# Landmark attention with a mixture of experts: a new order on VectorE, GpSimd and ScalarE in the query stage

## The chip, the core and the metric

The kernel runs on one core of a Trainium2 chip. The metric is the device time of one execution in microseconds (us), lower is better. Engines are TensorE (PE in the profile), VectorE (DVE), ScalarE (ACT), GpSimd (POOL) and SyncE (SP), which issues the DMAs here. Each runs its own list of instructions in order; semaphores tie them together.

## What is computed

Eight sequences of 2048 tokens with 256 channels go through a kernel attention with 64 landmarks per head (16 heads) and a layer norm, and then through a top-2 mixture of 8 experts and another layer norm:

```python
Phi_Q = jnp.exp(-C_Q / temperature)        # squared distances of queries to 64 landmarks
...
Y = jnp.linalg.solve(W_kernel, Z)
out_unnorm = jnp.einsum('bhnk,bhkd->bhnd', Phi_Q, Y)
norm = jnp.einsum('bhnk,bhko->bhno', Phi_Q, jnp.linalg.solve(W_kernel, Phi_K_sum))
out = out_unnorm / jnp.maximum(norm, 1e-10)
...
x = _layernorm(x + attn(x))
# ffn: logits = x @ Wg.T + bg; top 2 of 8 experts, softmax of the two logits
all_out = jnp.einsum('nd,ehd->neh', xf, We) + be
out = jnp.sum(sel * gate_w[:, :, None], axis=1)
x = _layernorm(x + out)
```

## The kernel before

The key stage (some 680 us) builds the landmark sums and inverses. It isn't touched. The query stage behind it works through 32 chunks of 512 tokens, four chunks a batch. A chunk is four tiles of 128 tokens. All its engine lists are written out by hand, so the order of the calls in the code is the order on the engine.

The stage is a software pipeline. One turn of the loop handles three chunks at once: p is in the experts, c = p + 1 in normalisation and gates, q = p + 2 in distances and attention.

TensorE computes 16 expert products per chunk (`experts(p, n)`, n = 4t + pair for tile t and pair of experts), each of six matrix products (L299 to L301) into bank 2 or 3 in turn. Between them stand: the distances of q (L1606), the attention of q in two halves (L1636), the output projection, the transposes (L1662), the gate logits of c (L1674), the norms of queries (L1417), the transposes of the gates (L1683) and the bias term (L1694), which closes the chunk.

A tile's expert results are gathered so. VectorE takes the first pair out of bank 2 with the gates (`combine`, L1298 and L1299) into y_out, which frees the bank for the third pair. ScalarE weighs the other three pairs (`weigh`, L841) into three buffers; there are two sets of these, for even and odd tiles. GpSimd adds the three up (`sum_parts`, L561 to L563). VectorE adds that sum to y_out and takes its statistics (`finish`, L1306 to L1310). GpSimd turns statistics into coefficients (`ln2`, through L527 to L530, the second being a power). ScalarE applies them (`result`, L849). SyncE stores two tiles at a time.

VectorE has much more to do: it clamps phi (`q_clamp`, L1177), which the attention of that half waits for; it takes reciprocals of the norms in two halves and multiplies (`norm_begin`, L1199 and L1200; `norm_end`, L1206 and L1209); it adds the residual and takes the first norm's statistics (`residual_stats`, L1218 to L1226); it splits x1 (`x1_lo`, L1234) and the queries (L969) into high and low parts; it turns logits into gates (`gates_begin`, L1245 to L1259, with a cast at L1256; `gates_end`, L1266 to L1275). GpSimd also makes low parts (`split_lo`, L536; `attn_lo`, L542), adds the output bias to x_tok (`residual`, L549) and makes the first norm's coefficients (`ln1`). ScalarE also exponentiates the distances (L786), rounds the attention for `attn_lo` (`attn_hi`, L794) and normalises x1 (L808).

## Time and profile before

| | |
|---|---|
| median of 3 runs | 2023.41 us |
| lowest, highest | 2021.66, 2028.81 us |
| the profiled execution, its own time | 2032.55 us |
| its span | 2030.8 us |
| granted TensorE clock over the span | 0.952 |
| busy over the span: TensorE, VectorE, ScalarE, GpSimd | 1811.0, 1534.3, 1225.9, 931.6 us |

The trace shows for each instruction its start, its length and, in brackets, the idle time in front of it on its engine with what ended that. A chunk of the query stage takes 40 to 44 us. The chunk that is followed below begins with expert product 0 on TensorE at 1200.27 us and ends where the next begins, at 1240.18.

### The profile page before, as it was taken

Reading aid. Unit: us, or ns where it says so; the run is one execution under the profiler, and the core shown is the slowest. Engines: PE = TensorE matmul, PEld = TensorE weight load, DVE = VectorE, ACT = ScalarE, POOL = GpSimd, SP = SyncE. Lnnn points to the kernel's source line nnn. Section 1 sums busy time; section 2 is a strip of 40 time slices with the busy share of each in tenths; the row PEclk is TensorE's granted clock in tenths of the full one; section 3 lists DMA queues with packets and bytes.
Section 4 is the critical chain, followed back from the end, with each engine's and each line's share of the span. In section 5 each row is a group of like instructions: output and inputs, shape, how many; then the busy total and the mean of one; then the engine's idle time right before and its main releaser. Section 6 shows DMA issues by size and latency. Waiting matters only on the chain.

```text
span 2030.8 us, 42773 instructions
## 1 busy us (share of the span) xinstructions
PE 1811.0 (89%) x16312; PEld 1369.3 (67%) x16312; DVE 1534.3 (76%) x3316; ACT 1225.9 (60%) x2411; POOL 931.6 (46%) x1179
## 2 busy tenths in 40 slices
PE   4668999989884899999999999999999999999997
PEld 3267778878772676676667767667676667766765
DVE  5668854888434788888888888887888878888874
ACT  2246665766655466568557566655855756675553
POOL 2300000000001376666666677656766666666666
PEclk8689999999996899999999999999999999999999
DMA  2586696766955233333243333333324333333300
GB/s 81 78 179 144 159 199 142 179 160 166 196 146 142 68 82 96 89 90 88 73 109 93 80 94 78 96 87 94 89 73 105 87 91 90 77 86 92 89 27 21
DMA packets 210753, 214.02 MB, mean 105 GB/s; under 512 B 59228, under 2 KB 142580, under 8 KB 210292
## 3 DMA queue, kind: packets, MB, share of 16 engines
q1 hardware_dynamic: 210356, 210.75, 43.0%
q8 instruction: 129, 2.11, 0.4%
q14 instruction: 76, 0.62, 0.1%
q0 software_dynamic: 192, 0.52, 0.1%
HBM read 61.26 MB, written 23.59 MB: 42 GB/s over the span
## 4 chain that ended last, share of the span: by engine, by line
PE 42%; DVE 26%; POOL 12%; issue 10%; SPq 5%; DMA 3%; ACT 2%; DVEq 0%; POOLq 0%; ACTq 0%
PE bank L299 9%; PE bank L300 9%; PE bank L301 9%; POOL x_tok L549 3%; PE bank L1606 3%; PE bank L1496 3%; PE bank L1636 2%; POOL part_x L562 2%; POOL part_x L561 2%; DVE phi L1177 2%; PE bank L1512 2%; DVE nrm L1199 2%; PE bank L1497 2%; DVE if L1256 2%; DVE inversion L1053 2%
## 5 line engine op out<-in xcount | busy, mean ns | idle before, releaser
L299 PE MATMUL bank<-weh,x1h 128*128 128x512 f32 x1024 | 433.3, 423 | 36.8 <-DVE y_out L1299 17.6
L300 PE MATMUL bank<-weh,x1l 128*128 128x512 f32 x1024 | 408.9, 399 | 0.0
L301 PE MATMUL bank<-wel,x1h 128*128 128x512 f32 x1024 | 408.6, 399 | 0.0
L549 POOL TENSOR_TENSOR x_tok<-x_tok,bo_sb 128x1024 f32<-128x1024 f32 x32 | 76.8, 2401 | 531.7 <-DMA x_tok<-in_x 531.7
L841 ACT ACTIVATE part_x<-bank,gate 128x256 f32<-128x256 f32 x512 | 211.3, 477 | 171.0 <-PE bank L301 166.9
L299 PEld LDWEIGHTS bank<-weh,x1h 128*128 128x128 f32 x1024 | 195.2, 191 | 156.3 <-issue 60.5
L786 ACT ACTIVATE phi<-bank,nlt_cur,invt 128x512 f32<-128x512 f32 x256 | 187.0, 793 | 86.5 <-PE bank L1606 86.5
L301 PEld LDWEIGHTS bank<-wel,x1h 128*128 128x128 f32 x1024 | 195.3, 191 | 47.8
L641 ACT ACTIVATE phi<-bank,invt 128x512 f32<-128x512 f32 x256 | 162.6, 684 | 105.2 <-PE bank L1497 105.0
L300 PEld LDWEIGHTS bank<-weh,x1l 128*128 128x128 f32 x1024 | 195.9, 191 | 34.2
L561 POOL TENSOR_TENSOR part_x<-part_x 128x512 f32<-128x512 f32 x128 | 177.8, 1389 | 32.6 <-ACT part L841 32.4
L1025 DVE TENSOR_SCALAR phi<-phi,phi_max,phi_min 128x1024 f32<-128x1024 f32 x128 | 103.7, 810 | 105.3 <-ACT phi L641 105.2
L542 POOL TENSOR_TENSOR attn_l<-attn,attn_h 128x512 fp32r<-128x512 f32 x64 | 85.3, 1333 | 210.2 <-ACT attn_h L794 210.2
L841 ACT ACTIVATE part<-bank,gate 128x256 f32<-128x256 f32 x256 | 107.7, 479 | 121.1 <-PE bank L301 120.7
L1496 PE MATMUL bank<-l_hh,k_hl 128*128 128x256 f32 x512 | 145.9, 316 | 39.1 <-DMA k_ha<-key_aug 26.5
L562 POOL TENSOR_TENSOR part_x<-part_x,part 128x512 f32<-128x512 f32 x128 | 173.0, 1351 | 10.0
L1177 DVE TENSOR_SCALAR phi<-phi,phi_max,phi_min 128x1024 f32<-128x1024 f32 x128 | 144.2, 1162 | 19.1 <-ACT phi L786 18.7
L1636 PE MATMUL bank<-phi,y_cur 128*32 128x512 f32 x1024 | 133.2, 641 | 12.6 <-issue 8.7
L1496 PEld LDWEIGHTS bank<-l_hh,k_hl 128*128 128x128 f32 x512 | 100.2, 196 | 54.8 <-DMA k_hl<-kl 33.6
L1497 PE MATMUL bank<-l_lo,k_ha 128*128 128x256 f32 x512 | 132.2, 289 | 0.0
L527 POOL TENSOR_TENSOR ve<-mv,cst 128x1 f32<-128x1 f32 (+1 forms) x160 | 46.6, 291 | 185.3 <-DVE mv L1310 112.9
L299 PE MATMUL bank<-xh,wh 128*128 128x512 f32 x260 | 107.4, 413 | 13.2 <-DVE xl L1045 6.9
(198 smaller groups left out, 4465.5 us busy)
## 6 DMA issues: line engine op xcount, KB each, us to landing
x_raw<-in_xT SPq DMA_DIRECT2D x64, 512.0 KB, 4.4
q_stack<-kh SPq DMA_DIRECT2D x256, 128.0 KB, 2.4
x_tok<-in_x SPq DMA_DIRECT2D x32, 512.0 KB, 3.9
q_stack<-kl SPq DMA_DIRECT2D x128, 128.0 KB, 2.4
q_stack<-key_aug SPq DMA_DIRECT2D x128, 128.0 KB, 2.5
k_hl<-attn_h SPq DMA_DIRECT2D x32, 256.0 KB
k_ha<-attn_h SPq DMA_DIRECT2D x32, 256.0 KB
k_hl<-attn_l SPq DMA_DIRECT2D x32, 256.0 KB
```

What stands on the lines that cost most here:

```text
L299: nc.tensor.matmul(outp, ah, bh, start=first, stop=False)
L300: nc.tensor.matmul(outp, al, bh, start=False, stop=False)
L301: return nc.tensor.matmul(outp, ah, bl, start=False, stop=last)
L561: own.then(nc.gpsimd.tensor_tensor(a[0], a[0], a[1], ALU.add))
L562: own.then(nc.gpsimd.tensor_tensor(a[0], a[0], a[2], ALU.add))
L641: nc.scalar.activation(phi[:, n], bank[6 + s][:], ACT.Exp, scale=invt[:]).then_inc(exp_done, 1)
L786: nc.scalar.activation(phi[:, i], bank[6 + i % 2][:], ACT.Exp, bias=nlt_cur[:, i:i + 1], scale=invt[:]).then_inc(qexp_done, 1)
L841: last = nc.scalar.activation(parts[t % 2][q - 1][:, u * D:(u + 1) * D], bank[2 + q % 2][:, u * D:(u + 1) * D], ACT.Copy, scale=gate[at][: ...
L1177: V.tensor_scalar(two, two, phi_max[:], phi_min[:], ALU.min, ALU.max).then_inc(qphi_ready, 2)
L1496: mm(dst, k_hl[at][:, g, tok], wide(hh), start=True, stop=False)
L1497: last = mm(dst, k_ha[at][:, g, tok], wide(lo), start=False, stop=True)
L1636: last = mm(dst[32 * j:32 * j + 32, :], y_cur[:, 4 * half + j, n:n + 32], phi[:, 4 * half + j], start=True, stop=True)
```

## The change

On GpSimd the first norm's coefficients (`ln1(c)`) move behind `sum_parts(p, 0)`; `sum_parts(p, 1)` and `attn_lo(q, 0)` move ahead of `ln2(p, 0)` and of `residual(q)`; and `ln2` handles two tiles in one call: tiles 0 and 1 in one, tiles 2 and 3 of the chunk before in another. On VectorE, `combine(p, 0)` now stands ahead of `finish(p-1, 2)`, and `finish(p-1, 3)` stands behind the residual and `combine(p, 1)`. On ScalarE `result(p, 0)` stands next to `result(p, 1)`, and `result` for tiles 2 and 3 is put into the next turn, behind `weigh(p, 7)`. SyncE stores tiles 2 and 3 in the next turn. TensorE's list is as before.

```diff
@@ SyncE
+            def store_rows(p, half):
+                sp.wait_ge(res_ready, TPC * p + 2 * half + 2)
+                sp.dma_start(out_v[p, :, 2 * half:2 * half + 2],
+                             y_out[p % 2][:, 2 * half:2 * half + 2]).then_inc(res_stored[p % 2][half], 16)
...
+                    if p:
+                        store_rows(p - 1, 1)
                     stack_queries(p + 3)
...
-                    for half in range(2):
-                        sp.wait_ge(res_ready, TPC * p + 2 * half + 2)
...
+                    store_rows(p, 0)
@@ GpSimd
             def ln2(p, t):
-                pool.wait_ge(ln2_stats, TPC * p + t + 1)
-                layernorm_coefs(mv2, ve2, rs2, nt2, nm2, slice(t, t + 1)).then_inc(ln2_coef, 1)
+                pool.wait_ge(ln2_stats, TPC * p + t + 2)
+                layernorm_coefs(mv2, ve2, rs2, nt2, nm2, slice(t, t + 2)).then_inc(ln2_coef, 2)
...
                     sum_parts(p, 0)
+                    ln1(c)
+                    if p:
+                        ln2(p - 1, 2)
                     split_lo(q + 1, 1)
+                    sum_parts(p, 1)
+                    attn_lo(q, 0)
                     ln2(p, 0)
                     residual(q)
-                    sum_parts(p, 1)
-                    ln2(p, 1)
-                    attn_lo(q, 0)
                     sum_parts(p, 2)
                     attn_lo(q, 1)
                     sum_parts(p, 3)
-                    ln2(p, 2)
-                    ln2(p, 3)
-                    ln1(c + 1)
@@ ScalarE
-                if not first:
-                    result(p - 1, 2)
                 q_exps(p + 2, range(2, 4))
...
                     weigh(p, 7, me)
+                    if p:
+                        result(p - 1, 2)
+                        result(p - 1, 3)
                     x1_hi(c, nxt)
...
                     gate_exp(c)
-                    result(p, 0)
...
                     weigh(p, 14, me)
+                    result(p, 0)
                     result(p, 1)
...
-                    result(p, 3)
@@ VectorE
                 add_bias(p, at)
+                combine(p, 0, at)
                 if not first:
                     finish(p - 1, 2)
-                combine(p, 0, at)
+                residual_stats(p + 1, 1 - at)
+                combine(p, 1, at)
                 if not first:
                     finish(p - 1, 3)
-                residual_stats(p + 1, 1 - at)
-                combine(p, 1, at)
                 q_clamp(p + 2, range(0, 2))
```

The line numbers of the changed kernel are 5 to 7 higher. On GpSimd the middle of a turn, from behind `split_lo`, reads before as follows: coefficients of tile 0, x_tok (`residual`), the sum of tile 1, coefficients of tile 1, `attn_lo`.

```order
L536 TENSOR_TENSOR xl1<-x_raw0,xh1 128x1024 [waits xqh_ready]
L527 TENSOR_TENSOR ve2<-mv2,cst 128x1 [waits ln2_stats]
...
L549 TENSOR_TENSOR x_tok<-x_tok,bo_sb 128x1024 [waits xt_loaded]
L561 TENSOR_TENSOR part_x<-part_x 128x512 [waits part_ready]
L562 TENSOR_TENSOR part_x<-part_x,part 128x512 [waits pool_step]
L563 TENSOR_TENSOR part_x<-part_x 128x256 [waits pool_step]
...
L542 TENSOR_TENSOR attn_l<-attn,attn_h 128x512 [waits attnh_ready]
L561 TENSOR_TENSOR part_x<-part_x 128x512 [waits part_ready]
```

The same place in the changed kernel, from the coefficients of the two norms ahead of `split_lo` (ve1 is `ln1`, ve2 is `ln2`):

```order
L533 TENSOR_TENSOR ve1<-mv1,cst 128x4 [waits ln1_stats]
...
L533 TENSOR_TENSOR ve2<-mv2,cst 128x2 [waits ln2_stats]
...
L542 TENSOR_TENSOR xl1<-x_raw0,xh1 128x1024 [waits xqh_ready]
L567 TENSOR_TENSOR part_x<-part_x 128x512 [waits part_ready]
...
L548 TENSOR_TENSOR attn_l<-attn,attn_h 128x512 [waits attnh_ready]
L533 TENSOR_TENSOR ve2<-mv2,cst 128x2 [waits ln2_stats]
...
L555 TENSOR_TENSOR x_tok<-x_tok,bo_sb 128x1024 [waits xt_loaded]
L567 TENSOR_TENSOR part_x<-part_x 128x512 [waits part_ready]
```

Both norms' coefficients of eight instructions now stand ahead of xl1, and the x_tok addition stands where `attn_lo` stood, directly behind the coefficients of tile 1.

On VectorE, from the residual to the attention's norms (L1199), before:

```order
L1306 TENSOR_TENSOR y_out<-y_out,part_x 128x256 [waits comb_done,part_sum]
L1308 BN_STATS st2<-y_out 128x6 [waits acc_done]
L1310 BN_AGGR mv2<-st2 128x2 [waits dve_step]
L1218 TENSOR_TENSOR x1_0<-bank0,x_tok 128x256 [waits wo_done,xb_ready]
...
L1298 SCALAR_TENSOR_TENSOR y_spare<-bank2,gate1,x1_1 128x256 [waits res_stored10,be_added,ffn_done]
L1299 SCALAR_TENSOR_TENSOR y_spare<-bank2,gate1,y_spare 128x256 [waits dve_step]
L1177 TENSOR_SCALAR phi<-phi,phi_max,phi_min 128x1024 [waits qexp_done] x3
L1199 TENSOR_SCALAR nrm<-bank5 128x512 [waits attn_ready,out_done]
```

And in the changed kernel:

```order
L1225 TENSOR_TENSOR x1_0<-bank0,x_tok 128x256 [waits wo_done,xb_ready]
...
L1305 SCALAR_TENSOR_TENSOR y_spare<-bank2,gate1,x1_1 128x256 [waits res_stored10,be_added,ffn_done]
L1306 SCALAR_TENSOR_TENSOR y_spare<-bank2,gate1,y_spare 128x256 [waits dve_step]
L1313 TENSOR_TENSOR y_out<-y_out,part_x 128x256 [waits comb_done,part_sum]
L1315 BN_STATS st2<-y_out 128x6 [waits acc_done]
L1317 BN_AGGR mv2<-st2 128x2 [waits dve_step]
L1184 TENSOR_SCALAR phi<-phi,phi_max,phi_min 128x1024 [waits qexp_done] x3
L1206 TENSOR_SCALAR nrm<-bank5 128x512 [waits attn_ready,out_done]
```

The three instructions of `finish(p-1, 3)` have moved from in front of the residual to between the combination of tile 1 and the clamps.

## Rows read from the trace of the kernel before

**Rows 1.** A query-stage stretch: busy PE, PEld, DVE, ACT, POOL; clock, DMA

```profile
1200.00:1400.00 200.00, 191.57 (x1085) 140.47 (x1084) 164.62 (x395) 129.83 (x272) 137.85 (x177) 0.98 0.36 91
```

**Rows 2.** TensorE's waits, 720 to 1985 us: total, times, longest

```profile
PE bank L299 <- DVE y_out L1299: 15.1, 10, 2.1
PE bank L299 <- DVE y_spare L1299: 13.9, 13, 2.1
PE bank L1683 <- DVE g_st L1275: 13.2, 14, 1.4
PE bank L1636 <- issue: 8.7, 7, 2.5
PE bank L1674 <- DVE x1l L1234: 5.2, 14, 1.9
...
PE bank L1636 <- DVE phi L1177: 2.9, 4, 0.8
```

**Rows 3.** VectorE's waits in the same stretch

```profile
DVE y_spare L1306 <- POOL part_x L563: 52.4, 30, 2.9
DVE y_out L1306 <- POOL part_x L563: 48.3, 31, 4.5
```

**Rows 4.** Timeline of TensorE in one chunk: start, length, idle before

```profile
1215.00 1.92 PE L1636 MATMUL bank<-phi,y_cur 128*32 128x512 f32 x16
...
1226.19 0.17 PE L1674 MATMUL bank<-wg_s,x1h 128*128 128x16 f32 x1
...
1235.84 0.50 PE L299 MATMUL bank<-weh,x1h 128*128 128x512 f32 x1 [0.78 <-DVE y_out L1299]
```

**Rows 5.** Timeline of VectorE in the same chunk

```profile
1206.11 0.42 DVE L1306 TENSOR_TENSOR y_spare<-y_spare,part_x 128x256 f32<-128x256 f32 x1 [1.64 <-POOL part_x L563]
...
1211.37 0.48 DVE L1298 SCALAR_TENSOR_TENSOR y_out<-bank,gate,x 128x256 f32<-128x256 f32 x1 [0.75 <-PE bank L301]
...
1212.29 4.22 DVE L1177 TENSOR_SCALAR phi<-phi,phi_max,phi_min 128x1024 f32<-128x1024 f32 x3
...
1219.39 0.37 DVE L1306 TENSOR_TENSOR y_out<-y_out,part_x 128x256 f32<-128x256 f32 x1
...
1224.49 1.28 DVE L1234 TENSOR_TENSOR x1l<-bank,x1h 128x512 fp32r<-128x512 f32 x2
...
1228.31 0.43 DVE L1306 TENSOR_TENSOR y_out<-y_out,part_x 128x256 f32<-128x256 f32 x1 [1.22 <-POOL part_x L563]
...
1231.14 1.10 DVE L1256 CAST if<-i 128x8 f32<-128x8 uint32 x1
```

**Rows 6.** Timeline of GpSimd in the same chunk

```profile
1212.51 1.75 POOL L561 TENSOR_TENSOR part_x<-part_x 128x512 f32<-128x512 f32 x1
...
1217.07 2.40 POOL L536 TENSOR_TENSOR xl<-x_raw,xh 128x1024 fp32r<-128x1024 f32 x1
...
1222.44 2.41 POOL L549 TENSOR_TENSOR x_tok<-x_tok,bo_sb 128x1024 f32<-128x1024 f32 x1
...
1230.91 1.30 POOL L542 TENSOR_TENSOR attn_l<-attn,attn_h 128x512 fp32r<-128x512 f32 x1
```

**Rows 7.** Timeline, two other chunks: a GpSimd and two VectorE instructions

```profile
1257.75 2.40 POOL L536 TENSOR_TENSOR xl<-x_raw,xh 128x1024 fp32r<-128x1024 f32 x1
...
1259.30 1.13 DVE L1306 TENSOR_TENSOR y_spare<-y_spare,part_x 128x256 f32<-128x256 f32 x1
...
1359.63 1.26 DVE L1258 TENSOR_TENSOR oh<-cst,if 128x32 f32<-128x32 f32 x1
```

**Rows 8.** Timeline of ScalarE in the chunk followed

```profile
1210.65 0.85 ACT L841 ACTIVATE part<-bank,gate 128x256 f32<-128x256 f32 x2
...
1227.12 0.63 ACT L794 ACTIVATE attn_h<-attn 128x512 fp32r<-128x512 f32 x1
```

**Rows 9.** The power of the coefficients in the query stage: ns min/median/max, forms

```profile
L528 POOL TENSOR_TENSOR rs<-ve,cst x159: 545/550/1032, 700.3 to 2026.4; 128x1 f32<-128x1 f32 x128, 128x4 f32<-128x4 f32 x31
```

**Rows 10.** TensorE's busy time and clock, one stretch of two us

```profile
1644.00:1646.00 2.00, 2.00 (x10) 0.50 0.00 0
```

More of the change, by code:

```diff
@@ L478, in turn @@
                         sp.dma_start(x_raw[0][:], xT_v[:, :, bass.ds((p + 4) * CH, CH)]).then_inc(xq_loaded, 16)
-                    for half in range(2):
-                        sp.wait_ge(res_ready, TPC * p + 2 * half + 2)
-                        sp.dma_start(out_v[bass.ds(p, 1), :, 2 * half:2 * half + 2].rearrange("a p t d -> (a p) t d"),
-                                     y_out[p % 2][:, 2 * half:2 * half + 2]).then_inc(res_stored[p % 2][half], 16)
+                    store_rows(p, 0)
             for b in range(BATCH - 1):
@@ L486, in _ @@
             turn(BATCH - 1)
+            store_rows(NCH - 1, 1)
             for i in range(2):
@@ L576, in _ @@
             attn_lo(1, 1)
-            ln1(1)
             def turn(b):
@@ L600, in _ @@
             turn(BATCH - 1)
+            ln2(NCH - 1, 2)
         @block.scalar
@@ L882, in _, with first_tile @@
             attn_hi(1, 1)
-            def first_tile(p, at, first=False, new_batch=None):
+            def first_tile(p, at, new_batch=None):
                 q_exps(p + 2, range(0, 2))
@@ L890, in first_tile @@
                     z_landmark_major(new_batch)
-                if not first:
-                    result(p - 1, 2)
                 q_exps(p + 2, range(2, 4))
                 weigh(p, 3, at)
-            first_tile(0, 0, True)
+            first_tile(0, 0)
             def turn(b):
@@ L938, in _ @@
             turn(BATCH - 1)
+            result(NCH - 1, 2)
+            result(NCH - 1, 3)
         @block.vector
```

## The prediction

> **What bounds the kernel now.** I read the stretches first, then TensorE's waits, then one chunk's timeline on each engine. In the query stage (1200 to 1400 us) TensorE is busy for 191.57 us of 200, at a clock of 0.98, and VectorE for 164.62 [rows 1]. TensorE sets the time, and only its gaps can be won or lost. From 720 to 1985 us, some 30 chunks, it waited 15.1 + 13.9 us for VectorE's combination (L1299), 13.2 for the gates (L1683's releaser L1275), 8.7 + 2.9 before the attention products (L1636) and 5.2 before the gate logits (L1674) [rows 2]: 59.0 us, 1.97 per chunk. If all of it went, the kernel would take some 1964 us.
>
> VectorE waited 52.4 + 48.3 us for GpSimd's sums before `finish` (L1306) [rows 3], 3.3 per chunk. Those are the waits that the change goes for. They aren't TensorE's, so I followed one chunk. It begins on TensorE at 1200.27. Attention of half 0 runs from 1215.00 to 1216.92; I call its end E. The gate logits come at 1226.19 (E + 9.27), and expert product 14 could have started at 1235.84 - 0.78 = 1235.06 (E + 18.14) but waited for the combination of tile 3 [rows 4]. So each chunk has two legs. In leg A VectorE clamps phi just in time for the attention: TensorE went from distances to attention without an idle mark. In leg B VectorE starts at E and must reach `combine(p, 3)` by E + 18.14; it took 18.9.
>
> **Leg A: what is moved in front of the clamps.** In the tile-0 and tile-1 part `finish(p-1, 3)` stood before the residual. There it waited 1.64 us in the chunk shown, but in a place with slack: VectorE still waited 0.75 for TensorE before `combine(p, 1)` at 1211.37. This combination can't come earlier, since it needs expert product 4. Now `finish(p-1, 3)` stands behind it and in front of the three clamps that began at 1212.29 [rows 5]. It costs 0.43 for the addition and, to its last statistic, 1.2 in all. The clamps start at 1213.5. The first two free the attention. In the chunk shown they ended at 1215.0 because a GpSimd addition (1212.51, 1.75 long) held the second one back [rows 6]; GpSimd is again inside a sum there, so I keep that pattern. Attention starts 1.15 late: 1.15 us of TensorE wait, where L1636 now has 11.6 / 30 = 0.39. Bounds: 0 if the clamps then run unhindered, 1.7 if the second also meets a long addition.
>
> **Leg B: what goes and what comes.** Going: `sum_parts(p, 1)` is moved ahead of the coefficients and of the residual addition (2.41 us at 1222.44 [rows 6]), so `finish(p, 1)` loses its wait of 1.22 before 1228.31 [rows 5]. Alone this puts combine 3 at E + 17.7, and the expert wait is gone.
>
> Coming: GpSimd's instructions now lie elsewhere, and the trace shows that some VectorE instructions stand still while GpSimd runs one. The addition L1306 at 1259.30 took 1.13, ending 0.28 after GpSimd's `split_lo` (1257.75 + 2.40), against 0.37 at 1219.39. The tiny cast L1256 at 1231.14 took 1.10 and ended with `attn_lo` (1230.91 + 1.30). L1258, an operation on 32 numbers per partition at 1359.63, took 1.26 [rows 5 to 7]. A collision costs what is left of GpSimd's instruction, whatever VectorE's own length.
> The Trainium skill, page "SBUF — State Buffer", section "Who interferes with whom", says the same: two-input additions and casts in VectorE's fast modes block fully, they don't share. Were the port shared instead, each collision worked out below would cost half, the waits per chunk would be near 2.5 and the sum 2023 + 0.5 x 30 = 2038; by these rows it is the full block.
>
> The new GpSimd order, in the chunk's times: ScalarE's third weighing ended at 1211.5 [rows 8] and loses a 0.6 normalisation ahead of it, so `sum_parts(p, 0)` runs 1211.0 to 1215.5 (4.56 as before, 1212.51 to 1217.07 [rows 6]). Then `ln1(c)`, four short instructions whose power takes 1.03 for four columns [rows 9]: 1.85, plus 0.2 behind a clamp, to 1217.6. Then the two-column `ln2(p-1, 2)`: the power is 0.55 for one column and 1.03 for four, so I take 0.7, 1.45 in all, to 1219.05. Then `split_lo` to 1221.5. The new E is 1218.07, and `finish(p, 0)` comes 2.47 behind it as now (1219.39 - 1216.92), at 1220.54: it stands until 1221.8, 0.9 lost. GpSimd takes `sum_parts(p, 1)` straight behind, and its first addition holds the clamp of pairs 6 and 7 for 0.5. VectorE is now 1.4 late.
> - Gate logits: `x1_lo` ended at 1225.77, E + 8.85 [rows 5], and would end at E + 10.25; TensorE wants it at E + 9.27. Wait 1.0, now 0.17.
> - `finish(p, 1)`: it would come at E + 10.17 (1228.31 - 1.22) + 1.4 = 11.6. `attn_lo` follows ScalarE's rounding, 1227.75 or E + 10.83 [rows 8], and runs to E + 12.15. Blocked again; its statistics end at E + 13.15, where the chunk shown had 12.6. The wait removed is back as collisions.
> - The cast: before, GpSimd's coefficients started as soon as the statistics ended, and `attn_lo` started 2.60 after L1306 did; the cast came at 2.83. In the place of `attn_lo` now stands the residual addition, and the pow of two columns adds 0.15: 2.75 against 2.83. The cast thus stands behind 2.40 us, not 1.30: 1.3 more than in the chunk shown (if it slips in ahead, L1258 stands in its stead). Behind it `sum_parts(p, 2)` may catch L1258 for another 1.1, as at 1359.63.
>
> Combine 3 ends 6.3 behind the statistics in the chunk shown, now 7.6 to 8.7: E + 20.7 to 21.8. TensorE, 1.0 later by the logits, wants it at E + 19.15. Wait 1.55 to 2.65. The gates follow in the same order and cost no more (0.44 per chunk today goes into that wait).
>
> **The rest.** Coefficients for two tiles at a time save GpSimd 8 of 16 short instructions per chunk, some 2 us by [rows 9], but GpSimd isn't what TensorE waits for: 0, apart from the times above. On ScalarE two normalisations move behind the seventh weighing (1.1 us while it waits for the transposes; 0, at most 0.3 at x1_hi) and `result(p, 0)` next to `result(p, 1)` (0.5 before the last weighing; 0.6 of slack before product 1). On SP's queue the store of half 1 no longer stands ahead of the next x_tok load; it now stands ahead of `stack_queries` and waits for `result(p-1, 3)`, near E + 3.8, while the stacking needs rounded queries that come after the logits' time, E + 9: 0. Behind the last chunk both normalisations and the store follow the same last sum as before: within 1 us.
>
> **The sum.** TensorE's waits per chunk: 1.15 + 1.0 + 1.55 to 2.65 = 3.7 to 4.8, against 1.97. That is 1.7 to 2.8 more in 30 chunks, 52 to 85 us; middle 68. The profiled execution took 2032.55, 9 above the median of the timed ones; I put the difference on the median: 2023.4 + 68 = **2091**.
>
> **Rivals.**
> 1. The collisions don't line up. This is a race with a threshold: if `finish(p, 1)` is less than 0.7 late (collisions of `finish(p, 0)` and the clamp together), it passes before `attn_lo` starts. Then the coefficients wait for `attn_lo`, and the cast is through before the residual. Leg B's waits vanish, leg A's 1.15 stays: 0.8 less per chunk, 2023.4 - 25 = 1998; with a part of the chunks so, up to 2010. For it: VectorE's 3.3 us of waits do go. Against: `split_lo` would have to end 0.7 earlier than worked out. Chance 0.25.
> 2. Only the last collision is missed (the cast is free). Waits 1.15 + 1.0 + 0.2: 0.4 more, 2035; with half of leg A's delay lost too, no change. Chance 0.15.
> 3. The clock. In the chunk where TensorE waited 2.5 us before the attention, it ran at half its clock (0.50, that is 1.2 GHz) from 1644 to 1646 [rows 10]. Such stretches cost some 1.7 us each. With a wait near 2.5 in every chunk, a stretch in each costs up to 1.7 more for perhaps half of them in sight: 2091 + 25 = 2116. Chance 0.08.
> The Trainium skill, page "TensorE: Matmul & The Clock Gate", section "HAM oscillation — how this bites in real kernels", describes this: a kernel that waits in every tile can have its clock dropped in every tile. By that rule rival 3 would be the rule; the trace shows waits of 2.08 without a drop behind them.
>
> **Chances and range.** Forecast (2068 to 2108) 0.52. An effect under 0.5% (10 us) can't be told from none here. Faster by more than that: rival 1, 0.26. Within: 0.10, the lower part of rival 2. Slower: 0.64. The range must reach rival 1, whose time is 1998, and stops at 2112, leaving out the worst of rival 3. The forecast alone has 2068 to 2108.
>
> **What would show it.** Right: VectorE's wait for part_x before L1306 nearly gone; TensorE's wait before the attention near 1 us in most chunks; L1256's mean up from 1.1 towards 2.3; L1306 of `finish(p, 0)` over 1 us; waits before the gate logits and product 14. Wrong: L1256 under 0.5 and L1306 under 0.5 throughout (rival 1); an attention that starts without a wait, which would mean that the clamps aren't the last thing before it.

## The result, and the profile after

| | before | changed |
|---|---|---|
| median (lowest to highest) of 4 runs, us | 2024.39 (2021.66 to 2028.81) | 2072.22 (2068.61 to 2077.56) |
| span of the profiled execution, us | 2030.8 | 2068.9 |
| granted TensorE clock over the span | 0.952 | 0.947 |

The ratio is 1.0236, 95% interval 1.0206 to 1.0266: the change makes the kernel 2.4% slower. Lines of the changed kernel are 5 to 7 higher: L1306 is now the second instruction of `combine`, L1313 the addition of `finish`, L1184 the clamp, L1263 the cast, L1265 and L1266 the two comparisons behind it.

The same stretch as in [rows 1], with the same columns (TensorE, weight loads, VectorE, ScalarE and GpSimd busy; clock; DMA):

```profile
1200.00:1400.00 200.00, 185.50 (x1026) 136.07 (x1026) 164.81 (x379) 119.43 (x254) 116.89 (x121) 0.96 0.35 90
```

TensorE is busy for 6 us less of 200, and issues 1026 matrix products where it issued 1085. VectorE is as busy as before: it does less work in longer instructions. What TensorE waits for, 720 to 2020 us (total, times, longest), against [rows 2]:

```profile
PE bank L1681 <- DVE x1l L1241: 26.7, 22, 1.9
PE bank L299 <- DVE y_spare L1306: 15.4, 9, 2.4
PE bank L1643 <- DVE y_cur L1196: 15.4, 7, 2.2
PE bank L1690 <- DVE g_st L1282: 14.8, 17, 1.4
PE bank L1643 <- DVE phi L1184: 12.6, 22, 0.7
PE bank L299 <- DVE y_out L1306: 10.8, 5, 2.9
```

VectorE's waits for part_x, 100.7 us in [rows 3], are gone from the head of its list. It now waits for TensorE, which is itself late because of VectorE, as the list above shows:

```profile
DVE x L1225 <- PE bank L301: 53.8, 60, 2.1
DVE y_out L1305 <- PE bank L301: 41.2, 20, 3.2
DVE nrm L1206 <- PE bank L1643: 41.2, 29, 2.7
```

Now one chunk of the kind that the prediction followed. On TensorE, against [rows 4], three places with an idle mark:

```profile
1228.09 1.93 PE L1643 MATMUL bank<-phi,y_cur 128*32 128x512 f32 x16 [0.58 <-DVE phi L1184]
...
1240.61 0.28 PE L1681 MATMUL bank<-wg_s,x1h 128*128 128x16 f32 x1 [1.17 <-DVE x1l L1241]
...
1251.87 0.50 PE L299 MATMUL bank<-weh,x1h 128*128 128x512 f32 x1 [2.28 <-DVE y_out L1306]
```

VectorE there, against [rows 5]:

```profile
1224.76 0.41 DVE L1313 TENSOR_TENSOR y_spare<-y_spare,part_x 128x256 f32<-128x256 f32 x1
...
1225.88 2.88 DVE L1184 TENSOR_SCALAR phi<-phi,phi_max,phi_min 128x1024 f32<-128x1024 f32 x3
...
1232.48 1.88 DVE L1313 TENSOR_TENSOR y_out<-y_out,part_x 128x256 f32<-128x256 f32 x1
...
1241.80 0.70 DVE L1313 TENSOR_TENSOR y_out<-y_out,part_x 128x256 f32<-128x256 f32 x1
...
1244.89 0.17 DVE L1263 CAST if<-i 128x8 f32<-128x8 uint32 x1
1245.10 2.27 DVE L1265 TENSOR_TENSOR oh<-cst,if 128x32 f32<-128x32 f32 x1
1247.29 1.32 DVE L1266 TENSOR_TENSOR oh<-cst,if 128x32 f32<-128x32 f32 x1
```

GpSimd there, against [rows 6]:

```profile
1231.68 2.40 POOL L542 TENSOR_TENSOR xl<-x_raw,xh 128x1024 fp32r<-128x1024 f32 x1
...
1240.92 1.30 POOL L548 TENSOR_TENSOR attn_l<-attn,attn_h 128x512 fp32r<-128x512 f32 x1 [2.86 <-ACT attn_h L799]
1243.37 0.20 POOL L533 TENSOR_TENSOR ve<-mv,cst 128x2 f32<-128x2 f32 x1 [1.15 <-DVE mv L1317]
1243.64 0.71 POOL L534 TENSOR_TENSOR rs<-ve,cst 128x2 f32<-128x2 f32 x1
...
1244.92 2.40 POOL L555 TENSOR_TENSOR x_tok<-x_tok,bo_sb 128x1024 f32<-128x1024 f32 x1
1247.28 1.29 POOL L567 TENSOR_TENSOR part_x<-part_x 128x512 f32<-128x512 f32 x1
```

Read the last two fences side by side, by ends. L1313 starts 0.80 behind `split_lo` and ends at 1234.36, 0.28 after `split_lo` ends (1234.08). L1265, 32 numbers per partition, starts 0.18 behind the x_tok addition and ends at 1247.37, 0.05 after that ends. L1266 does the same with the first addition of the sum: 1248.61 against 1248.57. Beyond what they take when unhindered (0.41, 0.19 and 0.18), the three cost 1.5 + 2.1 + 1.1 us. Not every VectorE instruction does that: the norms' copy out of PSUM (1248.53, 0.68) and a reciprocal (1249.24, 1.75) ran at their usual length beside the rest of the same sum, and so did the two instructions of a combination out of PSUM (1235.99, 0.47 and 1236.50, 0.48) beside the sum of tile 1.

How regular it is, the first comparison over all chunks (ns: minimum, median, maximum):

```profile
L1265 DVE TENSOR_TENSOR oh<-cst,if x32: 191/2242/2281, 676.4 to 2026.3; 128x32 f32<-128x32 f32 x32
```

Seven chunks, those in which the next batch's landmark values are taken in between the clamps, are another kind. There `finish(p, 1)` slips in ahead of `attn_lo` and the comparison is free, on VectorE:

```profile
1332.02 0.41 DVE L1313 TENSOR_TENSOR y_out<-y_out,part_x 128x256 f32<-128x256 f32 x1
...
1335.03 0.20 DVE L1265 TENSOR_TENSOR oh<-cst,if 128x32 f32<-128x32 f32 x1
1338.71 0.45 DVE L1273 TENSOR_SCALAR gs<-ge 128x4 f32<-128x4 f32 x1
1339.41 1.13 DVE L1275 TENSOR_TENSOR gw<-gw,ge 128x4 f32<-128x4 f32 x1
```

and the collisions sit one place further on, in `gates_end` (L1273 on), on operations on four numbers per partition, under the sum of tile 2. TensorE waits in these chunks for y_cur, 2.2 us in each of the seven, and some 1.0 for the gates.

The other chunks differ behind L1265. Where the sum of tile 2 then catches L1266 as well, as above, TensorE waits some 2.3 us for the combination. Where L1266 slips through (0.18), the sum catches `gates_end` instead in nine chunks, and TensorE waits 0.7 for the gates; in four it catches next to nothing, and the combination costs 1.1.

**A book for all kernels.** In the table, "waits" is the sum of TensorE's listed waits from 720 us to the end of the stage. "Clock" is my sum of (1 - granted clock) x 2 us over all stretches of two us from 690 us on. "Rest" is the span less both. The clock column also counts stretches in which TensorE waits or has ended (3 to 6 us of it lie behind the last product, and in some rows the last stretch, 1.0 us, is left out), so 1 us in it means nothing.

| kernel | ratio to before (95%) | span | waits | clock | rest |
|---|---|---|---|---|---|
| before | 1 | 2030.8 | 68.7 | 25.5 | 1936.6 |
| changed | 1.0236 (1.0206 to 1.0266) | 2068.9 | 100.2 | 38.7 | 1930.0 |
| r_late | 1.0742 (1.0705 to 1.0779) | 2173.9 | 145.1 | 112.5 | 1916.3 |
| r_half | 1.0313 (1.0277 to 1.0350) | 2091.0 | 113.0 | 51.3 | 1926.7 |
| r_gap | 1.0111 (1.0062 to 1.0160) | 2050.6 | 83.5 | 39.2 | 1927.9 |
| dve_before | 1.0178 (1.0138 to 1.0217) | 2056.6 | 80.1 | 44.5 | 1932.0 |
| clamp_first | 1.0212 (1.0181 to 1.0243) | 2066.3 | 85.1 | 31.4 | 1949.8 |
| fin_mid | 1.0196 (1.0170 to 1.0222) | 2058.8 | 80.1 | 49.3 | 1929.4 |
| gap_split | 1.0038 (1.0022 to 1.0055) | 2030.5 | 83.5 | 24.6 | 1922.4 |
| gap_split_mid | 0.9845 (0.9818 to 0.9873) | 1987.4 | 48.2 | 8.8 | 1930.4 |
| one_tile | 0.9872 (0.9838 to 0.9907) | 1999.3 | 48.6 | 16.6 | 1934.1 |
| gates_clear | 0.9652 (0.9630 to 0.9675) | 1958.1 | 22.0 | 6.7 | 1929.4 |
| after_clear | 1.0115 (1.0080 to 1.0150) | 2037.2 | 66.2 | 48.8 | 1922.2 |
| before_clear | 0.9861 (0.9827 to 0.9896) | 1989.1 | 43.6 | 15.4 | 1930.1 |

For twelve of the fourteen the rest is 1922 to 1937. So nearly all of each difference is in the two columns in the middle: of the change's 38.1 us of span, 31.5 are waits and 13.2 clock, and the rest fell by 6.6.

The 31.5 are made up of 21.5 more before the gate logits, 16.4 more before the attention (15.4 + 12.6 in place of 8.7 + 2.9) and 3.1 more for the gates, less 6.2 for the combinations (26.2 in place of 32.4 to the end of the stage) and 3.3 for ScalarE and the DMA.

### The profile page after: what moved, and what is told of

It is laid out like the page before. It is cut to its first block, busy times and chain, and to the rows that moved or that the text cites. A ratio compares the mean times of both kernels' runs of the same rounds, so it can differ in the third digit from the quotient of the medians.

```text
span 2068.9 us, 42581 instructions
## 1 busy us (share of the span) xinstructions
PE 1819.7 (88%) x16312; PEld 1373.4 (66%) x16312; DVE 1569.4 (76%) x3316; ACT 1227.7 (59%) x2411; POOL 874.2 (42%) x923
## 4 chain that ended last, share of the span: by engine, by line
PE 47%; DVE 31%; issue 12%; SPq 4%; ACT 2%; DMA 2%; POOL 1%; DVEq 0%; ACTq 0%; POOLq 0%
PE bank L299 10%; PE bank L300 9%; PE bank L301 9%; PE bank L1643 4%; PE bank L1503 2%; DVE y_spare L1313 2%; DVE nrm L1213 2%; PE bank L1519 2%; PE bank L1613 2%; DVE phi L1184 2%; PE bank L1504 2%; DVE inversion L1060 2%; DVE phi L1032 2%; DVE kl L976 2%; DVE st L1315 2%
## 5 line engine op out<-in xcount | busy, mean ns | idle before, releaser
L299 PE MATMUL bank<-weh,x1h 128*128 128x512 f32 x1024 | 432.9, 423 | 28.3 <-DVE y_spare L1306 15.4
L568 POOL TENSOR_TENSOR part_x<-part_x,part 128x512 f32<-128x512 f32 x128 | 178.7, 1396 | 10.0
L1032 DVE TENSOR_SCALAR phi<-phi,phi_max,phi_min 128x1024 f32<-128x1024 f32 x128 | 103.7, 810 | 100.5 <-ACT phi L646 100.3
L1643 PE MATMUL bank<-phi,y_cur 128*32 128x512 f32 x1024 | 141.9, 678 | 28.5 <-DVE y_cur L1196 15.9
L1184 DVE TENSOR_SCALAR phi<-phi,phi_max,phi_min 128x1024 f32<-128x1024 f32 x128 | 121.3, 981 | 18.3 <-ACT phi L791 17.7
L299 PE MATMUL bank<-xh,wh 128*128 128x512 f32 x260 | 107.8, 415 | 13.2 <-DVE xl L1052 6.9
L1207 DVE RECIPROCAL nrm<-nrm 128x256 f32<-128x256 f32 x64 | 112.2, 1753 | 2.2
```

The lines of the kernel that those rows point to most:

```text
L299: nc.tensor.matmul(outp, ah, bh, start=first, stop=False)
L568: own.then(nc.gpsimd.tensor_tensor(a[0], a[0], a[2], ALU.add))
L1184: V.tensor_scalar(two, two, phi_max[:], phi_min[:], ALU.min, ALU.max).then_inc(qphi_ready, 2)
L1643: last = mm(dst[32 * j:32 * j + 32, :], y_cur[:, 4 * half + j, n:n + 32], phi[:, 4 * half + j], start=True, stop=True)
```

## Experiments

The theory: the change costs what VectorE stands still behind GpSimd's long instructions. The main rival: it costs what the moved `finish(p-1, 3)` and the new order on VectorE make late by themselves. All edits are to the changed kernel unless said otherwise.

### The x_tok addition: smaller, or elsewhere

Three ways to free L1265. **r_half** cuts the addition in two, the halves on either side of the sum:

```diff
-                    residual(q)
+                    half_residual(q, 0)
                     sum_parts(p, 2)
+                    half_residual(q, 1)
```

> The changed kernel with the x_tok addition cut into two halves of 512 columns, one where the whole stood, one behind the sum of tile 2. The total work on GpSimd grows only by one instruction's fixed cost. Theory (the hold lasts for what is left of the GpSimd instruction): L1265 falls by half, to about 1.1 us, followed by a hold of up to 1.3 on the next one as before; VectorE is 1.1 us earlier per chunk, time about 2072 - 25 = 2047. If VectorE's loss didn't depend on the length of the instruction it meets, the median would stay at 2.2 and the time at 2072.

Measured: 2092.26 us. The dose came out: this comparison, L1281 here, took half of its 2242 ns.

```profile
L1281 DVE TENSOR_TENSOR oh<-cst,if x32: 191/1142/1168, 671.9 to 2047.4; 128x32 f32<-128x32 f32 x32
```

The time did not fall to the 2047 that I expected: the second half now stood in front of the gates, where TensorE's wait rose from 14.8 to

```profile
PE bank L1706 <- DVE g_st L1298: 50.3, 29, 2.5
```

**r_late** puts the whole addition behind the sum of tile 2:

```diff
-                    residual(q)
                     sum_parts(p, 2)
+                    residual(q)
```

> The changed kernel with GpSimd's x_tok addition (residual of q, 2.40 us) moved behind the sum of tile 2. Theory (collisions with GpSimd's long addition hold VectorE's small gate operations, 2.27 us in 23 of 30 chunks): L1265's median falls from 2.24 to about 0.2, TensorE's waits before product 14 (15.4 + 10.8 us) and for g_st (14.8) go almost entirely, the waits before the gate logits (26.7) and the attention (28) stay; time 2072 - 40 = 2032. Rival (VectorE is late in leg B for other reasons, its wait is only named here): waits unchanged, 2072. Rival (the place behind the sum collides with something as costly): 2060 or more.

Measured: 2175.82 us, the slowest of all, and 144 off what I expected. L1265 was free (median 192 ns). The collision had moved whole, to an instruction of `gates_end`, median 2303 ns. Ahead of it the sum held L1273 for 1.27 as well:

```profile
L1276 DVE TENSOR_TENSOR oh<-oh,gw x32: 191/2303/2304, 676.3 to 2134.3; 128x32 f32<-128x32 f32 x32
```

Behind it TensorE waited for the gates 28 times up to 2020 us, 2.8 us each. One such wait, and the clock in the stretches from 1246 on (TensorE busy, weight loads, VectorE, ScalarE, GpSimd, clock, DMA):

```profile
1246.24 0.61 PE L1690 MATMUL bank<-cst,g_st 128*24 128x128 f32 x4 [2.82 <-DVE g_st L1282]
```

```profile
1246.00:1248.00 2.00, 1.76 (x9) 1.43 (x10) 1.93 (x6) 1.11 (x3) 0.00 (x0) 0.81 0.03 8
1248.00:1250.00 2.00, 2.00 (x7) 1.20 (x5) 1.49 (x3) 2.00 (x6) 0.00 (x0) 0.50 0.44 102
1250.00:1252.00 2.00, 2.00 (x6) 1.54 (x6) 1.18 (x4) 0.40 (x1) 1.52 (x2) 0.50 0.95 180
1252.00:1254.00 2.00, 2.00 (x6) 1.60 (x5) 0.92 (x3) 0.00 (x0) 1.92 (x2) 0.50 0.77 224
1254.00:1256.00 2.00, 2.00 (x13) 1.70 (x12) 1.26 (x4) 0.79 (x2) 1.17 (x2) 0.99 0.78 281
```

Six us at 1.2 GHz in place of 2.4: this wait of 2.8 cost about 3.4 more in clock. Over the stage the clock column went from 38.7 to 112.5. So of r_late's 105 us of span above the changed kernel, 45 are waits and 74 clock (the rest fell by 14).

The waits of 2.8 us are only half of that clock. Low stretches stand behind 17 of the 28, at 1.7 or 3.4 us each; with the last one of 3.3 us they make up 55 of the 112.5. Another 43 stand behind the waits of some 1.2 us before the gate logits, such as this one:

```profile
1231.41 0.28 PE L1681 MATMUL bank<-wg_s,x1h 128*128 128x16 f32 x1 [1.18 <-DVE x1l L1241]
```

```profile
1234.00:1236.00 2.00, 2.00 (x16) 0.36 (x8) 1.72 (x19) 0.00 (x0) 1.30 (x4) 0.50 0.87 201
```

In r_late all 21 of these have a low stretch behind them, in the changed kernel 10 of 22. The length of the last wait alone therefore doesn't decide whether the clock falls; what else does, these runs don't show.

**r_gap** puts it where GpSimd was idle for 2.86 us, ahead of `attn_lo`:

```diff
                     sum_parts(p, 1)
+                    residual(q)
                     attn_lo(q, 0)
                     ln2(p, 0)
-                    residual(q)
                     sum_parts(p, 2)
```

> The changed kernel with the x_tok addition between the sum of tile 1 and attn_lo, where GpSimd stood idle for 2.87 us in each chunk while VectorE runs reciprocals and operations with an input from PSUM. Theory of collisions: no VectorE instruction of the two-input SBUF or cast kind meets the 2.40 us, L1265 falls to 0.2 and L1273 to L1276 meet at most the sum of tile 2; the waits before product 14 go, the one for g_st is under 1 us, so the clock isn't dropped as in the run with the addition behind the sum (waits of 2.8, clock 0.916). Gate logits (1.17) and attention (0.57) waits stay. Time 2072 - 35 = 2037, 2020 to 2045. If the clock dropped for another reason than long waits, it would stay near 0.92 and the time above 2100.

Measured: 2047.22 us, 25 below the changed kernel, 10 above my middle value and 2 outside my range. L1265 took 191 ns (median) and the waits for the combination fell from 26.2 us to

```profile
PE bank L299 <- DVE y_spare L1306: 0.6, 1, 0.6
```

The sum of tile 2 had moved 2.4 us forward, though, and met L1273 (median 1278 ns in place of 456): the wait for the gates rose from 14.8 to 23.6. Three runs, one answer: a collision costs what is left of GpSimd's instruction, and when that instruction moves, the cost moves to whatever stands there. Only a place where VectorE has nothing that collides would be free.

### What stands before the attention

**dve_before** gives VectorE its old order:

```diff
+                if not first:
+                    finish(p - 1, 2)
                 combine(p, 0, at)
                 if not first:
-                    finish(p - 1, 2)
+                    finish(p - 1, 3)
                 residual_stats(p + 1, 1 - at)
                 combine(p, 1, at)
-                if not first:
-                    finish(p - 1, 3)
```

> VectorE's list as in the kernel before; GpSimd, ScalarE and SyncE as in the changed kernel. Theory (leg A's loss comes from finish(p-1, 3) in front of the clamps): the wait before the attention for phi, 12.6 us in 22 waits of 0.57, falls below 5 us; VectorE waits again before L1306. Leg B is unchanged or slightly worse, since split_lo comes as late as before and E earlier: gate logits and product 14 keep their waits. Time 2060 to 2072. Rival (the VectorE order is the main cause of the slowdown): 2035 or less.

**clamp_first** moves `finish(p-1, 3)` alone, behind the second half's clamps:

```diff
                 combine(p, 1, at)
-                if not first:
-                    finish(p - 1, 3)
                 q_clamp(p + 2, range(0, 2))
@@ in the turn
                     q_clamp(q, range(2, 4))
+                    if p:
+                        finish(p - 1, 3)
@@ behind the last turn
+            finish(NCH - 1, 3)
```

> The changed kernel with finish(p-1, 3) behind the second clamp instead of in front of the first. Theory: the phi wait before the attention goes (12.6 us); against it stands that ScalarE's fifth weighing now waits for that finish, some 1.3 us longer, and delays the normalised rows by up to 1. Time 2060 to 2072. Rival (the 0.57 wait is the end of a chain that is hidden anyway by leg B): 2072 exactly, as waits in leg B grow by what leg A gives.

**fin_mid** moves it one place, in front of `combine(p, 1)`:

```diff
                 residual_stats(p + 1, 1 - at)
-                combine(p, 1, at)
                 if not first:
                     finish(p - 1, 3)
+                combine(p, 1, at)
                 q_clamp(p + 2, range(0, 2))
```

> The changed kernel with finish(p-1, 3) between the residual statistics and combine(p, 1), in the 1.95 us that VectorE waits there for product 4. Theory of leg A: the wait before the attention for phi (12.6 us) and most of the one for y_cur (15.4 to about 7) go, without the waits for GpSimd that the kernel before had. Leg B's waits stay as they follow the attention. Time 2072 - 15 = 2057. Rival (leg B takes back what leg A gives, since GpSimd's split_lo is bound to weighings before E): 2065 to 2072.

Measured: 2060.68, 2069.62 and 2063.02 us. In all three the wait for phi went (0.5, 0 and 0 us), and the one for y_cur fell from 15.4 to 6.7 or 6.6. So leg A costs what `finish(p-1, 3)` costs in front of the clamps: 0.57 us in 22 chunks, and (15.4 - 6.7) / 7 = 1.24 in the seven others. But of those 21 us only 3 to 12 came back. In dve_before and fin_mid leg B got later: the wait for the gate logits, 26.7 us in the changed kernel, is 37.3 in fin_mid, and in dve_before

```profile
PE bank L1681 <- DVE x1l L1241: 36.5, 22, 1.9
```

What leg A gains, leg B takes back: when attention starts 0.57 earlier, E moves, GpSimd's `split_lo` does not, and `finish(p, 0)` stands that much longer behind it. In the changed kernel `split_lo` starts 1.67 us after E in the ordinary chunks, and that addition takes 1.88. In fin_mid it starts 2.25 after E, and

```profile
1225.18 2.46 DVE L1313 TENSOR_TENSOR y_out<-y_out,part_x 128x256 f32<-128x256 f32 x1
```

With it the wait before the gate logits is 1.74 in most ordinary chunks, where it was 1.17. So what I had named as the rival for fin_mid happened in most chunks; its time lies between mine (2057) and the rival's (2065 and more). In clamp_first the waits for the gate logits and for the combinations stayed (25.4 and 26.3), TensorE waited 7.2 us for ScalarE's x1, and the column "rest" rose by 20 us. Some 15 of these lie in the transposes of x1 on TensorE (L1670): in 22 chunks that wait cuts them in two, and up to the next product they take 1.67 us, 0.32 of it the wait, where the changed kernel has 0.79; in the seven others they take 1.2. The remaining 5 us are open.

The rival is down as the whole cause: put back alone, VectorE's order is worth at most 12 of the 48 us. It isn't nothing, though. Some 21 of leg A's 28 us of waits come from `finish(p-1, 3)` in front of the clamps, and once leg B's collisions are out of the way the same edit is worth far more (gap_split_mid, below).

### The collision at the head of leg B

**gap_split** adds to r_gap that `split_lo` goes ahead of the two-tile coefficients, so that it ends some 1.5 us sooner (four short instructions, 1.45 by the prediction):

```diff
                     ln1(c)
+                    split_lo(q + 1, 1)
                     if p:
                         ln2(p - 1, 2)
-                    split_lo(q + 1, 1)
                     sum_parts(p, 1)
+                    residual(q)
                     attn_lo(q, 0)
                     ln2(p, 0)
-                    residual(q)
```

> r_gap, with split_lo ahead of ln2(p-1, 2) on GpSimd. Theory: finish(p, 0) no longer meets split_lo (L1313 at 1.88 falls under 0.7), so the 1.17 wait before the gate logits (26.7 us in all) shrinks to under 0.3, and finish(p, 1) comes before attn_lo. Time that of r_gap less 25 to 35 us: about 2008. Rival (the gate logits wait for x1_hi on ScalarE, which comes later since the coefficients of tiles 2 and 3 do): wait stays at 1, time as r_gap or more.

Measured: 2032.3 us, 24 above what I expected. The gate logits' wait went as expected, from 26.5 to 1.9 us. In its place stood one that I had not foreseen, in the seven chunks, where y_cur had cost 15.4:

```profile
PE bank L1643 <- issue: 28.6, 7, 4.1
```

Its releaser isn't named, but VectorE and GpSimd show it in one of them: the second and third clamps, and `split_lo` at its new, earlier place.

```profile
1298.90 3.43 DVE L1184 TENSOR_SCALAR phi<-phi,phi_max,phi_min 128x1024 f32<-128x1024 f32 x2
```

```profile
1298.71 2.35 POOL L542 TENSOR_TENSOR xl<-x_raw,xh 128x1024 fp32r<-128x1024 f32 x1
```

Two clamps take 3.43 us where 1.54 stands in such a chunk of the changed kernel (1318.95 us): the second clamp waited out `split_lo`. The sum of TensorE's waits is the same 83.5 us as in r_gap; what gap_split gained on it, 20 us of span, is clock (14.6) and rest (5.5). With `finish(p-1, 3)` out of the way the clamps should come some 1.2 us earlier and miss it. That is **gap_split_mid**, gap_split with fin_mid's edit:

> All three moves together: x_tok addition in GpSimd's gap, split_lo ahead of ln2(p-1, 2), finish(p-1, 3) in VectorE's wait before combine(p, 1). Theory: all of TensorE's waits but the batch ones are small, sum under 25 us from 720 to 1985 against 65 before and 98 in the changed kernel; time 1985, that is faster than the kernel before by 40. If the earlier E makes finish(p, 0) meet split_lo again, 2010.

Measured: 1990.0 us, ratio 0.9845 (0.9818 to 0.9873). This beats the kernel before by 1.5%. The expected sum of waits did not come out (48.2, not under 25), mainly for the gates:

```profile
PE bank L1690 <- DVE g_st L1282: 28.0, 31, 1.5
```

The time nearly did (I expected 1985), as the clock column fell to 8.8, where the changed kernel has 38.7 and the kernel before 25.5. The three moves together bring 82 us. r_gap alone brings 25, `split_lo` on top of it 15, and fin_mid's edit, which alone brings 9, brings 42 on top of both: what is left on one leg hides what another move gives.

### The gates

Now one wait is left, under the sum of tile 2. **gates_clear** adds to gap_split_mid that this sum waits for the end of the gates, two lines on GpSimd:

```diff
+                    if not past_end(c):
+                        pool.wait_ge(gst_ready, c + 1)
                     sum_parts(p, 2)
```

> The three moves of gap_split_mid, and GpSimd's sum_parts(p, 2) also waits until VectorE has ended the gates (gst_ready). In gap_split_mid TensorE still waits 28.0 us in 31 places for the gates (g_st), and in the chunk shown gates_end's first instruction (L1273) takes 0.92 and its third (L1275) 0.57 while GpSimd is in the sum. Theory (the wait is made of collisions with this sum): L1273's median falls from over 0.4 us to 0.16, the g_st wait to under 8 us, and the time from 1990 to 1965-1975. The sum would end near 1220.5 in that chunk, and finish(p, 2) comes at 1222.4, so nothing waits for it. Rival (gates_end is late for another reason, the gates' chain on VectorE as a whole): L1273 falls but TensorE's g_st wait stays over 15 us and the time stays at 1985-1995. Second rival (a collision moved is a collision kept): the sum now stands under the attention's multiplication L1216 or the combination, and the wait returns there: time 1985 or more with another wait grown by 15 us.

Measured: 1954.96 us, ratio 0.9652 (0.9630 to 0.9675), the fastest. All 32 executions of the first gate instruction (L1273 in the changed kernel, L1275 here) are short now:

```profile
L1275 DVE TENSOR_SCALAR gs<-ge x32: 157/160/171, 682.5 to 1918.9; 128x4 f32<-128x4 f32 x32
```

The g_st wait isn't among TensorE's waits any more. The longest sum left is

```profile
PE bank L299 <- ACT part L848: 8.5, 7, 1.2
```

and GpSimd now idles in front of that sum:

```profile
POOL part_x L567 <- DVE g_st L1284: 158.3, 31, 8.7
```

With 158 us of waiting put on the engine that has time to spare, the kernel is 35 us faster than gap_split_mid.

**after_clear** and **before_clear** add the same two lines to the changed kernel and to the kernel before.

> The changed kernel, and GpSimd's sum_parts(p, 2) also waits until VectorE has ended the gates; none of the three moves. The changed kernel's TensorE waits are 26.7 us for x1_lo, 26.2 for the combinations, 15.4 for y_cur, 14.8 for g_st, 12.6 for phi. Theory (each collision has its own price): only g_st (14.8) and what the sum adds to L1266 (median of the third-from-last digit, up to 1.32 each, part of the 26.2) go; L1265 still stands 2.24 behind the residual addition, x1_lo and phi stay. Time 2072 - 15 to 25 = 2047-2057. Rival (the gates' collisions with this sum are the main loss of the change, and the rest is slack): time at or below 2030, as before the change.

> The kernel before, with that one wait added ahead of sum_parts(p, 2), nothing else changed. It tells whether the order of the change is needed for the gain of gates_clear (ratio 0.9652). In the kernel before TensorE waits 13.2 us for g_st and 32.4 for the combinations ahead of products, and L1256 takes a median of 1.10 behind attn_lo. Theory (the wait takes away only the collisions with this sum): g_st's 13.2 goes and a part of the combinations', time 2024 - 15 to 30 = 1995-2010. Rival (the old order with the wait is as good as the new one with three moves): 1955-1975, which would need the 32.4 us to go as well. Second rival (the sum delayed makes finish(p, 2) or attn_lo of half 1 late): 2020 or more, with waits for part_x or attn_l on the rise.

Measured: 2044.90 us (ratio 1.0115, 1.0080 to 1.0150) and 1994.35 (0.9861, 0.9827 to 0.9896), both just below the ranges that I had given (2047 to 2057, 1995 to 2010). In after_clear the wait for the gates is gone, and that for the combinations fell from 26.2 to 7.5; x1_lo (26.7), y_cur (15.4) and phi (12.6) stand to the digit as they were, and so does the comparison behind the x_tok addition:

```profile
L1267 DVE TENSOR_TENSOR oh<-cst,if x32: 191/2243/2285, 672.1 to 1995.1; 128x32 f32<-128x32 f32 x32
```

In before_clear the g_st wait is gone and the combinations wait 20.4 us, not 32.4, but `issue` and x1l are left:

```profile
PE bank L299 <- DVE y_out L1301: 10.4, 12, 1.0
PE bank L299 <- DVE y_spare L1301: 10.0, 12, 1.1
PE bank L1638 <- issue: 7.6, 7, 2.5
PE bank L1676 <- DVE x1l L1236: 5.2, 14, 1.9
```

So one wait of two lines gives the kernel before 1.4%, and the new order with the three moves and the wait gives 3.5%: with its long GpSimd instructions at other places and `finish(p-1, 3)` one place earlier, the order of the change beats the old one. Whether the old order with moves of that kind would do as well was not run.

### Two tiles at a time

**one_tile** is gap_split_mid with the second norm's coefficients one tile at a time:

```diff
             def ln2(p, t):
-                pool.wait_ge(ln2_stats, TPC * p + t + 2)
-                layernorm_coefs(mv2, ve2, rs2, nt2, nm2, slice(t, t + 2)).then_inc(ln2_coef, 2)
+                for i in (t, t + 1):
+                    pool.wait_ge(ln2_stats, TPC * p + i + 1)
+                    layernorm_coefs(mv2, ve2, rs2, nt2, nm2, slice(i, i + 1)).then_inc(ln2_coef, 1)
```

> The three moves of gap_split_mid with the second normalisation's coefficients one tile at a time, at the same two places. Each place has eight short instructions in place of four: some 0.8 us more of GpSimd. The prediction put the pairing at nothing, apart from the times. Behind attn_lo there is 1.19 us of idle time before the sum of tile 2, so nothing is expected there. Ahead of sum_parts(p, 1) the 0.8 us move this sum and the residual addition: in the chunk shown finish(p, 1) comes 0.08 behind the end of the residual, so it would meet 0.7 us of it. Theory (positions decide, not GpSimd's load): L1313 on y_out gets longer and the time rises by 5 to 20 us, to 1995-2010. Rival (pairing is worth nothing here): within 4 us of gap_split_mid, 1986-1994.

Measured: 1999.37 us, ratio 0.9872 (0.9838 to 0.9907), against 0.9845 (0.9818 to 0.9873). The time lies in the band that I gave, but the intervals overlap, and the sum of waits is the same (48.6 and 48.2). The median of the `finish` addition rose from 415 to 456 ns on y_out, where I had looked for it, and from 425 to 690 on y_spare, and the clock column from 8.8 to 16.6. Whether the pairing is worth 0.3% or nothing is left open; it isn't what moved the kernel.

## Why the prediction was right

The forecast was 2091 with a range of its own of 2068 to 2108, and the time 2072.22 lies in it, near its lower end. Most steps were found in the trace as they were put, and in the chunk that was followed TensorE's waits add up to 0.58 + 1.17 + 2.28 = 4.03 us, inside the 3.7 to 4.8; where the sum over all chunks was too high is told last.

- **The main wait gone, and worth nothing.** VectorE's 100.7 us of waits for part_x vanished, and TensorE's waits rose. Right: they weren't TensorE's.
- **`finish(p, 0)` behind `split_lo`.** Worked out 0.9 lost; 1.88 - 0.41 = 1.5 in the chunk shown. The clamp behind: 0.5 worked out, 0.99 - 0.8 = 0.2 found. Together 1.4 and 1.7. The gate logits' wait was put at 1.0 and is 1.17 (26.7 us in 22 chunks is 1.2). gap_split, with `split_lo` ended sooner, took it to 1.9 us in all: shown to be the cause.
- **`finish(p, 1)` behind `attn_lo`.** Its statistics were to end at E + 13.15. E is 1230.02 here and they end at 1243.28, E + 13.26. The addition took 0.70.
- **The race for the cast.** The margin was worked out as 2.75 against 2.83, 0.08 the other way: the cast won it by 0.03 (3.09 behind the start of L1313, the x_tok addition 3.12), and the next instruction took the whole 2.27, the case given in brackets. The sum of tile 2 then held L1266 for another 1.1, as in the upper bound. Product 14 waited 2.28, within 1.55 to 2.65. r_gap removes it: shown. The sign that I named, a longer cast, didn't come: its median fell to 171 ns, and it was caught in three chunks only (2.1 to 2.2 us).
- **The power of two columns.** Estimated at 0.7, measured 0.71.
- **ScalarE, SyncE, pairing at nothing.** ScalarE's first norm waited 0.96 us for GpSimd's coefficients in the chunk shown; TensorE's waits for ScalarE in the whole stage are 1.5 us (4.1 before): right as far as TensorE goes. The pairing: left open, above.
- **The Trainium skill,** page "SBUF — State Buffer", section "Who interferes with whom", says that of a VectorE and a GpSimd instruction which need the pair of ports that the two share, the later one is blocked fully and not slowed. The collisions looked at here are full blocks (2.27 for an operation whose minimum is 0.19, 1.14 when GpSimd's instruction was halved), so the trace and the runs agree with the page; half of each, by the prediction, would have given 2038.

**What was mis-sized.** The sum had 3.7 to 4.8 us of waits per chunk, 30 times, against 1.97: 52 to 85 more. Found were 31.5 us more.

- Leg A was put at 1.15 us of wait in all chunks, 34.5 in 30. Found are 28.0: 2.2 in seven, which had 8.7 in all before (`issue` in [rows 2]), and 0.57 in 22. The term took over the clamps' length of [rows 5], 4.22 for three, because GpSimd is again in a sum. Here they took 2.88: the second clamp began with less of GpSimd's instruction left. The step "I keep that pattern" failed; a collision's price hangs on tenths of a microsecond, and one chunk's pattern isn't kept when both lists move.
- The wait for a combination, 1.55 to 2.65, was counted in each chunk, 46 to 80 us. It comes 14 times and makes 26.2 us in all, below the 29.0 of [rows 2]: nine times 2.25 or more, four times 1.1, once 0.6. This is the term that was most in error. In the chunks with landmark values `finish(p, 1)` won its race against `attn_lo`, and rival 1's picture holds, as far as this leg goes: at 0.2 for L1265. In nine others L1266 slipped in ahead of the sum, which then held `gates_end`: a wait of 0.7 for the gates in place of 2.3 for the combination. The gates, for which the sum put nothing, got 16.3 us to the end of the stage. That the chunks with landmark values are a kind of their own could have been read from the trace of before, where `issue` comes 7 times.
- The gate logits were put at 1.0 in each chunk, 30 us, and found at 26.7: the seven chunks with landmark values have no such wait.
- Rival 3, the clock, came in part. It lost 38.7 us in place of 25.5: 13 us that the sum did not have. Before the change, too, 5 of the 11 waits of 2.08 us had a low stretch behind them; the prediction speaks of those without.
- The base. I put the difference on the median. The spans differ by 38.1 us and the medians by 47.8, since the profiled execution of before lay 8 us above its median and that of the changed kernel 1.5 below. So some 10 of the 47.8 us are in no pair of rows.

The sum had 36.5 us of waits too much (68 against 31.5), and lacked the 13 of the clock and the 10 of the base; the rest fell by 6.6. That the total is only 19 us off, and inside the range, is in part luck: these errors have opposite signs.

The Trainium skill, page "TensorE: Matmul & The Clock Gate", section "HAM oscillation — how this bites in real kernels", says that a kernel which waits in every tile can have its clock dropped in every tile. In the changed kernel it happened in some: of its 16 waits of 2.2 us or more, 7 have a low stretch behind them. Behind the 2.28 before 1251.87 the clock stayed at 1.00 through 1260; behind the 2.29 before 1207.24 it was 0.50 from 1208 to 1210. In r_late there was one behind 17 of 28 waits of 2.8 us and behind all 21 of some 1.2, and what the clock cost above the changed kernel (74 us) was more than what the waits did (45).

## What to carry to other kernels

When GpSimd and VectorE both work from SBUF, plan their lists together: beside each long GpSimd instruction write down which VectorE instruction with two SBUF inputs, cast or plain scalar operation, however small, will arrive during it, and put it where VectorE is busy with PSUM or with a reciprocal, or let GpSimd wait. A collision that is moved is not removed: test a move by the whole list of waits, not by the one instruction that it frees, and expect several moves to pay only together. Before multiplying one chunk's collisions by the number of chunks, look at each kind of chunk.

## What the runs showed of the hardware that I had not expected

- Operations on four numbers per partition are held too. L1273, 158 ns alone, took 1278 ns (median in r_gap) beside a 1.28 us GpSimd addition; L1275, 163 ns alone, up to 1122 ns in gap_split_mid.
- VectorE gets through between two GpSimd instructions. In the chunk shown, L1265 and L1266 ended within 0.05 us of the ends of two successive GpSimd instructions (1247.32 and 1248.57), one each.
- GpSimd is held as well: the power of four columns took 1.46 us at 1228.18, where the third clamp still ran, where 1.03 is its time in [rows 9].
- The clock can take away nearly as much as the waits do: 112.5 us beside 145.1 of waits in r_late, 38.7 beside 100.2 in the changed kernel. Half-clock stretches came behind waits of only 1.2 us as well, 21 of 21 in r_late and 10 of 22 in the changed kernel. In gates_clear, with 22 us of waits in all, 6.7 us are left.
